# Block quantization in two sublayers: a software pipeline over VectorE and ScalarE, and one reciprocal in place of two operations on the thresholds

## What is computed

```
x = x + 0.5 * ffn(layernorm(x))
x = x + attn(layernorm(x))        # retention with 8 heads, silu gate
x = x + 0.5 * ffn(layernorm(x))

def ffn(x):                       # x: 2048 x 1024 on each core
    xq, xs = mx_quantize(x)       # blocks of 32 along a row
    wq, ws = mx_quantize(weight)  # 1024 x 1024
    return (xq * xs) @ (wq * ws).T + bias

def mx_quantize(t):
    scale = max(max(|block of 32|) / 7.5, 1e-30)
    q = nearest value of a 6-bit grid (step 1/8 below 2, 1/4 below 4, 1/2 up to 7.5)
    return q, scale               # a tie goes to the lower value
```

## Time and profile before

| | |
|---|---|
| median of three runs | 1972.01 us |
| profiled execution | 1973.91 us, span of its slowest core 1972.3 us |
| spans of the eight cores | 1962.9 to 1972.3 us |
| VectorE busy | 1153.9 us, 59% |
| TensorE matmul busy | 770.0 us, 39% |
| ScalarE busy | 423.0 us, 21% |
| first sublayer | from 34 to 618 us, of which weight stage 77 to 234 |
| second layernorm, projections, retention, output projection | 618 to 1518 us |
| second sublayer | 1518 to 1943 us |
| output DMAs | 1943 us to the end |

### The profile page before, as it was taken

How to read it: one execution, slowest core, us unless ns; L and a number is a source line. 1 busy time by engine, 2 the same in 40 slices (tenths; PEclk the granted TensorE clock), 3 DMA queues, 4 the chain that set the end, 5 groups by cost and what they waited for, 6 DMA issues and landing times.

```text
span 1972.3 us, 15241 instructions; the slowest of 8 cores (1962.9 to 1972.3 us)
## 1 busy us (share of the span) xinstructions
PE 770.0 (39%) x3776; PEld 355.3 (18%) x3776; DVE 1153.9 (59%) x1635; ACT 423.0 (21%) x1302; POOL 20.8 (1%) x41
## 2 busy tenths in 40 slices
PE   0000033233331339578694554455547032333331
PEld 0000011111110114233242222223213011111110
DVE  0499999999993214230105555555522399999992
ACT  2400000000004620002234444444401500100000
POOL 0000000000000100000000000000001000000000
PEclk9999975665665559788896777777769556656665
DMA  6010100000000353431100000000044000000004
GB/s 203 11 32 22 43 0 0 1 0 0 0 0 0 107 169 152 170 139 53 65 1 1 1 1 1 1 1 1 1 142 157 0 0 0 0 0 0 0 0 170
DMA packets 18852, 81.26 MB, mean 41 GB/s; under 512 B 2000, under 2 KB 2000, under 8 KB 16464
## 3 DMA queue, kind: packets, MB, share of 16 engines
q1 hardware_dynamic: 11904, 53.02, 8.1%
q0 software_dynamic: 6864, 27.27, 4.0%
HBM read 61.41 MB, written 18.87 MB: 41 GB/s over the span
## 4 chain that ended last, share of the span: by engine, by line
DVE 46%; PE 26%; ACT 10%; issue 8%; DMA 5%; DVEq 1%; SPq 1%; ACTq 0%; POOL 0%; POOLq 0%
DVE arena L60 46%; PE psc L60 20%; ACT arena L60 10%; PE pbig L60 4%; PE pt L60 2%; DVEq L68 1%; DMA arena<-wo 1%; DMA arena<-wq 1%; DMA arena<-wk 1%; DMA arena<-ident 1%; DMA arena<-wv 1%; SPq L60 1%; DMA arena<-wg 1%; ACTq L68 0%; POOL out L60 0%
## 5 line engine op out<-in xcount | busy, mean ns | idle before, releaser
L60 PE MATMUL psc<-arena 128*128 128x512 bf16 x2112 | 590.6, 436 | 136.4 <-DVE arena L60 115.5
L60 PE MATMUL pt<-arena 128*128 128x128 bf16 x576 | 130.3, 265 | 1031.1 <-DVE arena L60 968.5
L60 DVE TENSOR_SCALAR arena<-arena 128x1024 f32<-128x1024 f32 (+4 forms) x378 | 193.5, 530 | 272.3 <-ACT arena L60 184.0
L60 ACT COPY arena<-pt 128x128 bf16<-128x128 bf16 x576 | 132.7, 267 | 944.6 <-PE pt L60 944.0
L60 DVE TENSOR_TENSOR arena<-arena 128x1024 f32<-128x1024 f32 (+3 forms) x347 | 285.6, 823 | 37.3 <-DVE arena L60 1.4
L60 DVE SCALAR_TENSOR_TENSOR arena<-arena 128x1024 f32<-128x1024 f32 (+3 forms) x251 | 289.3, 1152 | 27.3 <-DVE arena L60 0.9
L60 PEld LDWEIGHTS psc<-arena 128*128 128x128 bf16 x2112 | 222.2, 108 | 431.2 <-issue 271.9
L60 PEld LDWEIGHTS pt<-arena 128*128 128x128 bf16 x576 | 60.3, 105 | 1110.0 <-issue 1098.1
L60 DVE TENSOR_TENSOR arena<-psc,arena 128x128 bf16<-128x128 f32 (+1 forms) x192 | 81.3, 424 | 177.2 <-PE psc L60 163.1
L60 ACT CAST arena<-psc 128x512 bf16<-128x512 f32 (+1 forms) x224 | 106.1, 496 | 295.5 <-PE psc L60 252.8
L60 DVE CAST arena<-arena 128x1024 int32<-128x1024 f32 (+1 forms) x80 | 55.4, 694 | 151.9 <-PE psc L60 57.8
(11 more groups left out here) (12 smaller groups left out, 80.5 us busy)
## 6 DMA issues: line engine op xcount, KB each, us to landing
arena<-x SPq DMA_DIRECT2D x4, 2048.0 KB, 19.5
xspill<-arena POOLq DMA_DIRECT2D x16, 512.0 KB, 3.4
arena<-qsc SPq DMA_DIRECT2D x8, 1024.0 KB, 4.9
arena<-ksc SPq DMA_DIRECT2D x8, 1024.0 KB, 5.2
arena<-xspill POOLq DMA_DIRECT2D x16, 512.0 KB, 4.0
out<-arena POOLq DMA_DIRECT2D x4, 2048.0 KB, 16.1
arena<-wf SPq DMA_DIRECT2D x8, 512.0 KB, 3.8
arena<-wq SPq DMA_DIRECT2D x8, 512.0 KB, 4.7
```

The source lines that it names most:

```text
L60: inst = getattr(getattr(self.nc, eng), name)(*a, **k)
```

## The change

`quant_tile` is split into stages, and the two loops become a software pipeline in which a chunk's second half stands in the queue after the next chunk's first.

- `q_stageA` (VectorE): block maximum, scale, reciprocal of the scale, y.
- `q_yy` (ScalarE, new there): y squared by `activation` with `Square`.
- `q_B1` (VectorE): the compares, now with results -4 and -2; one operation adds 8, which gives the inverse of the step directly (8, 4 or 2); y times that; then a `reciprocal` of the whole 128x1024 tile gives the step.
- `q_cast` (ScalarE, new there): float32 to int32.
- `q_B2` (VectorE): the same seven last operations as before, in other buffers.
- `x_d` (ScalarE, new there): x minus mean by `activation` with `Identity` and the bias `negm_sb`, two chunks ahead. One 128x16 operation per sublayer computes `negm_sb`.

In the x loop the queue of VectorE is A(rc), B2(rc-1), evacuation(rc-2), B1(rc); that of ScalarE is square(rc), cast(rc), x_d(rc+2), copies(rc-1). PE's transposes wait for the last operation of B2 alone. Block results are double-buffered.

```diff
-            c.op("vector", "scalar_tensor_tensor", qb1, qby, 0.0, qby,
-                 ALU.bypass, ALU.mult).inc("v")
-            c.wait("vector", "v")
-            c.op("vector", "tensor_scalar", qb0, qb1, 4.0, 0.125, ALU.is_ge,
+        def q_yy(p, y_v):
+            c.wait("scalar", "v", y_v)
+            c.op("scalar", "activation", qb1, qby_y[p], AF.Square).inc("s")
+            return c.cnt["s"]
+
+        def q_B1(p, yy_s):
+            c.wait("vector", "s", yy_s)
+            c.op("vector", "tensor_scalar", qb2, qb1, 4.0, -4.0,
+                 ALU.is_ge, ALU.mult).inc("v")
+            c.op("vector", "tensor_scalar", rb_buf, qb1, 16.0, -2.0,
+                 ALU.is_ge, ALU.mult).inc("v")
+            c.wait("vector", "v")
+            c.op("vector", "scalar_tensor_tensor", qb2, qb2, 8.0, rb_buf,
+                 ALU.add, ALU.add).inc("v")
+            c.wait("vector", "v")
+            c.op("vector", "tensor_tensor", qby_y[p], qby_y[p], qb2,
                  ALU.mult).inc("v")
-            c.op("vector", "tensor_scalar", qb2, qb1, 16.0, 0.25, ALU.is_ge,
+            tq_v = c.cnt["v"]
+            c.wait("vector", "v")
+            c.vsync(c.op("vector", "reciprocal", qb2, qb2))
+            return tq_v
+
+        def q_cast(p, tq_v):
+            c.wait("scalar", "v", tq_v)
+            c.op("scalar", "copy", qbi, qby_y[p]).inc("s")
+            return c.cnt["s"]
...
-            c.op("vector", "scalar_tensor_tensor", qb1, qb0, 0.125, qb2,
-                 ALU.add, ALU.add).inc("v")
-            c.op("vector", "tensor_scalar", qb3, qb2, -8.0, 8.0, ALU.mult,
-                 ALU.add).inc("v")
-            c.wait("vector", "v")
-            c.op("vector", "scalar_tensor_tensor", qb0, qb0, -32.0, qb3,
-                 ALU.mult, ALU.add).inc("v")
-            c.wait("vector", "v")
-            c.op("vector", "tensor_tensor", qby, qby, qb0, ALU.mult).inc("v")
-            c.wait("vector", "v")
-            c.op("vector", "tensor_copy", qbi, qby).inc("v")
...
+            def x_d(rc, guard_v):
+                c.wait("scalar", "v", guard_v)
+                c.op("scalar", "activation", db[rc % 2], x_sb[:, rc, :],
+                     AF.Identity, bias=negm_sb[:, rc:rc + 1]).inc("s")
+                sd[rc] = c.cnt["s"]
...
+            x_d(0, max(negm_v, w_end_v))
+            x_d(1, max(negm_v, w_end_v))
             for rc in range(RC):
...
+                c.wait("vector", "s", sd[rc])
+                xy[rc] = q_stageA(rc % 2, db[rc % 2], ln_rstd[:, rc:rc + 1])
+                xyy[rc] = q_yy(rc % 2, xy[rc])
+                if rc >= 1:
+                    x_B2(rc - 1)
                 if rc >= 2:
...
+                    ffn_evac(rc - 2)
+                xtq[rc] = q_B1(rc % 2, xyy[rc])
+                xcast[rc] = q_cast(rc % 2, xtq[rc])
+                if rc + 2 < RC:
+                    x_d(rc + 2, xxd[rc - 1] if rc >= 1 else xy[rc])
                 if rc >= 1:
...
+                    s_after = x_tr(rc - 1)
+                    x_mm(rc - 1, s_after)
+            x_B2(RC - 1)
+            ffn_evac(RC - 2)
+            s_after = x_tr(RC - 1)
+            x_mm(RC - 1, s_after)
             ffn_evac(RC - 1)
```

More of the change, by code:

```diff
@@ L178, in build_program @@
     zrow_sb = [vbf(O_C + 10368, 128), vbf(O_C + 10624, 128)]
+    negm_sb = vf32(O_C + 10880, 16)
     sem_ctx = ExitStack()
@@ new lines, in q_stageA @@
+            rsb = rs.unsqueeze(2).broadcast_to([128, 32, 32])
+            if rstd_c is not None:
+                c.op("vector", "scalar_tensor_tensor", b32(qby_y[p]),
+                     b32(src2d), rstd_c, rsb, ALU.mult, ALU.mult).inc("v")
+            else:
+                c.op("vector", "tensor_tensor", b32(qby_y[p]), b32(src2d),
+                     rsb, ALU.mult).inc("v")
+            return c.cnt["v"]
+        def q_yy(p, y_v):
+            c.wait("scalar", "v", y_v)
+            c.op("scalar", "activation", qb1, qby_y[p], AF.Square).inc("s")
+            return c.cnt["s"]
@@ L285, in quant_tile @@
[L285 to L293, removed]
+            sclb = q_scl2[p].unsqueeze(2).broadcast_to([128, 32, 32])
@@ L310, in ffn_sublayer, with w_dma, w_B2, w_tr @@
             ln_stats(x_sb, EPS_LN)
+            c.op("vector", "tensor_scalar", negm_sb[:, 0:16], ln_mean, -1.0,
+                 None, ALU.mult).inc("v")
+            negm_v = c.cnt["v"]
+            global qby_y, rb_buf, cm_buf
             if build_wdt:
+                qby_y = [qby, qb3]
+                rb_buf = qb0
+                cm_buf = qb0
+                wy = {}; wyy = {}; wtq = {}; wcast = {}; wxd = {}
+                wtr = {}
+                dma_here = {}
+                def w_dma(jc):
+                    st = wst_sb[jc % 2]
+                    wsem = "wa" if jc % 2 == 0 else "wb"
+                    if jc >= 2:
+                        c.wait("sync", "v", wy[jc - 2])
+                    c.wait("sync", wsem)
+                    c.op("sync", "dma_start", out=st,
+                         in_=w_dr["wf"][jc * 128:(jc + 1) * 128, :]).inc(wsem, 16)
+                    dma_here[jc] = c.cnt[wsem]
+                def w_B2(k):
+                    xg = wtr[k - 2] if k >= 2 else 0
+                    wxd[k] = q_B2(k % 2, wcast[k], ffntmp, wdrow_sb[k % 2], xg)
+                def w_tr(k):
+                    c.wait("tensor", "v", wxd[k])
+                    transpose_1024(wdrow_sb[k % 2],
+                                   lambda kc, jj=k: wdt_sb[:, kc,
+                                                          jj * 128:(jj + 1) * 128])
+                    wtr[k] = c.cnt["t"]
+                for jc in range(2):
+                    w_dma(jc)
                 for jc in range(KC):
@@ L336, in ffn_sublayer, with x_B2, x_tr, x_mm @@
                 c.wait("tensor", "ld")
+                w_end_v = c.cnt["v"]
+            qby_y = [qby, qb3]
+            db = [qb0, wst_sb[1]]
+            rb_buf = wst_sb[0]
+            cm_buf = wst_sb[0]
+            sd = {}; xy = {}; xyy = {}; xtq = {}; xcast = {}; xxd = {}
+            tr_done = {}
             ev_done = {}
             mm_done = {}
-            tr_done = []
+            def x_d(rc, guard_v):
[3 more added lines that the diff above has]
+                sd[rc] = c.cnt["s"]
+            def x_B2(k):
+                xg = tr_done[k - 2] if k >= 2 else 0
+                xxd[k] = q_B2(k % 2, xcast[k], db[(k + 1) % 2],
+                              xdrow_sb[k % 2], xg)
+            def x_tr(k):
+                c.wait("tensor", "v", xxd[k])
+                s_after = transpose_1024(
+                    xdrow_sb[k % 2],
+                    lambda kc, rr=k: xdt_sb[:, kc, rr * 128:(rr + 1) * 128])
+                tr_done[k] = c.cnt["t"]
+                return s_after
+            def x_mm(k, s_after):
+                fp = psc[:, (k % 2) * 1024:(k % 2) * 1024 + 1024]
+                c.wait("tensor", "s", s_after)
+                if k >= 2:
+                    c.wait("tensor", "v", ev_done[k - 2])
+                for jh in range(2):
+                    for kc in range(KC):
+                        ins = c.op("tensor", "matmul",
+                                   fp[:, jh * 512:(jh + 1) * 512],
+                                   xdt_sb[:, kc, k * 128:(k + 1) * 128],
+                                   wdt_sb[:, kc, jh * 512:(jh + 1) * 512],
+                                   start=(kc == 0), stop=(kc == KC - 1),
+                                   skip_group_check=True)
+                        if jh == 1 and kc == KC - 1:
+                            ins.inc("t")
+                mm_done[k] = c.cnt["t"]
             def ffn_evac(rc):
```

126 lines of the change are left out of this document (49 added, 77 removed).

## The result

The changed kernel takes 2058.91 us (median of nine runs), against 1972.12 us for the kernel before on the same chips: ratio 1.0447, 95% interval 1.0426 to 1.0469. That is +86.8 us where +79.5 were forecast, 2058.9 where 2051.5 were, inside the range of 2036 to 2070.

A forecast was written before the change was run, and what follows sets the result against it. VectorE's queue was taken to bound the quantizing loops. Weight chunks +19.3, x chunks +55.4 and edges +4.8 us sum to +79.5 us: 1972.0 becomes 2051.5 us, range 2036 to 2070.

The forecast's parts named there:

- The bound: Quantizing stages: time is the sum of VectorE's queue, start to start; 19.56 us a weight chunk, 23.30 an x chunk.
- The reciprocal's price: B1's new 128x1024 reciprocal: 6.25 ns a column from three narrow ones, 6553 ns, 6.65 us with the gap.
- The rival in which it streams like a product: Wide reciprocal in B1 costs only 1.22 us, so the kernel gets faster, 1838 us; chance 5%.
- the one in which its price rises with width: Wide reciprocal in B1 costs up to 11.3 us, kernel 2240 us at that bound; chance 4%.
- The figure of eight repeats: Alternative reciprocal estimate from the skill page: eight cycles, 8.33 ns a column, about 8.7 us a tile, about 2137 us.
- What left the queue: VectorE per chunk: square 1.33, thresholds 1.94, cast 0.79, x subtraction 0.86 us; saved 4.24 (weight, with 0.18 waits), 4.92 (x).
- the sum: VectorE's queue per chunk after the change: 21.97 us a weight chunk, 25.03 an x chunk.
- The cover of ScalarE's trips: Steady chunks: ScalarE trips of 1.26 us stay hidden behind VectorE's work, with about 4.7 us to spare for the square.
- The edges: Loop starts and ends: uncovered ScalarE waits and negm_sb, less 5.0 us of transpose waits; together +4.8 us.
- the waits: VectorE's wait gaps: B1 loses one (-0.18 us a chunk), the evacuation gains one (+0.18 an x chunk).

The follow-up runs named there:

- four edits of that queue: Changed kernel, reciprocal replaced by two operations: 1876.08 us, or by one int32 operation: 1823.24; kernel before, threshold part alone: 2173.83; changed kernel, square on VectorE: 2107.06 profiled.
- the fused repair: Changed kernel with int32 step, reordered waits, earlier first subtraction, plus rounding repair in three operations instead of five: 1767.99 us, ratio 0.8959 to the kernel before.
- the halves: Changed kernel with the 1024-column reciprocal taken as two of 512 columns: 2056.32 us, one execution.
- the serial kernel: Kernel before with only the threshold part changed, wide reciprocal included, no pipeline: 2173.83 us, ratio 1.0995.
- The wait order experiment: Changed kernel with VectorE's wait for its own last result placed last ahead of stage A and B2: 2055.18 us, one execution.

## Why the prediction was right

- **The bound.** VectorE's queue was the time of the loops: four edits of that queue (-4.53, -5.86, +4.71, +1.33 us a chunk) moved the loops by what forty of them sum to, within 2 us (the last less the 3.5 us of three waits for the square that it takes away). The bound gives way only in the fused repair, where 1.40 us less a chunk brought 48 us of 56, because TensorE's matmuls came to be waited for.
- **The reciprocal's price** from the slope of three narrow ones: forecast 6553 ns, measured 6553. It decided the sign. The rival in which it streams like a product, and the one in which its price rises with width, fell with that row and with the halves.
- **The figure of eight repeats** in the Trainium skill ("VectorE: DVE Perf Modes", section "Walkthrough: the 8-slice pipeline in each mode") is a repeat count and no price: read as eight cycles for a column it would have given 2137 us. The trace bears out 6.25 ns, which is six cycles of the 0.96 GHz that the page states.
- **What left the queue**: square, pair of the thresholds, cast, subtraction at their start-to-start times. The square was undone alone and gave its 1.33 us back, and the threshold part was taken alone in the serial kernel. Cast and subtraction were not tried alone; they stand in the sum that the period bears out.
- **The cover of ScalarE's trips**: right. The trips for square and cast lay in the shadow in the steady chunks also where the chunk had shrunk to 17.8 us. What ran out there was the room between the end of the matmuls and the evacuation (6.57 us or more in the changed kernel, nothing in 65 evacuations of the fused one).
- **The edges**: forecast +4.8 us, with waits for ScalarE at the loops' starts and 5.0 us less waiting for TensorE at their ends (18.2 us before, 13.4 after). The loops' +84.5 less 8 x (22.04 - 19.56) = 19.8 and 32 x (25.18 - 23.30) = 60.2 leaves 4.5, or 4.2 when the weight chunks from the fourth on are taken at their 22.10 us.
- **The step that was mis-sized: the waits.** The prediction counted B1's missing wait at -0.18 us and the evacuation's new one at +0.18, and no change for stage A and B2. Each of these got one more wait behind the blocking one, 0.07 us each: 0.14 us in an x chunk, 0.07 in a weight chunk and 0.14 from the fourth on, some 5 us in all. That is the difference between 79.5 and the 84.5 us of the loops. The wait order experiment shows the mechanism; the periods became the 25.04 us (25.03 in the sum) and 21.97 us that the sum had.
- The other 2.3 us of the 86.8 lie outside the loops, where nothing was changed. They are within what the middle varies from trace to trace; no experiment was made on them.

The case in one line: the pipeline and the algebra were sound, they take 97 us from the loops of the kernel before when the step is made by two ordinary operations (868.7 against 965.4), and the one operation that stood in their place cost 40 x 6.65 = 266 us where the two cost 40 x 2.12 = 85.

## What to carry to other kernels

Where one engine's queue is the time, price each instruction by kind, not by count: take the slope of the narrow ones in the trace and carry it to the new width before an operation is used at that width. A value that is always a power of two has a cheaper inverse than a reciprocal. When an instruction has several waits, put the one that really blocks last. And the arithmetic of one queue ends where the chain of another engine becomes as long: look each time at how much room the other engines have left.

## What the runs showed of the hardware

- VectorE's reciprocal of float32 took 153 ns + 6.25 ns a column at 8, 16, 32, 512 and 1024 columns (203, 253, 353, 3353 and 6553 ns); a product takes 1.04 ns a column (167 ns at 8, 1225 at 1024).
- A tensor_scalar from int32 to int32 with multiply and add over 1024 columns took 694 ns, nearly as little as the float32 form (688 ns).
- One wait in program order behind the one that blocks added some 0.07 us to VectorE's start (a gap of 0.17 us for 0.10); the same wait ahead of it added nothing. More than one behind was not tried.
- ScalarE's cast from float32 to int32 took 1045 ns for 128x1024, VectorE's 694 (0.69 us in the earlier trace rows).
- Idle stretches of VectorE of 0.44 to 0.53 us, with nothing awaited, stood 128 of its instruction records or a multiple of it apart in the loops of all twelve traces, 4 to 8 on each core.
- The 16 matmuls of a chunk took 5.35 us at a mean granted clock of 0.67 and 6.50 us at 0.55, between the levels of 1.2 and 2.4 GHz (0.5 and 1).
